# Two interleaved recurrences: products that use the same weights share one weight load on TensorE

## What is computed

```
# layer 1, state h1 (2 x 256), for each position
gate = sigmoid(h1 @ Wh + x_t @ Wz + b)
h1 = tanh(h1 * leak + gate * x_t)
# layer 2, a gated recurrent unit, state h2 (2 x 256), for each position
z  = sigmoid(x_t @ W_z + h2 @ U_z + bias_z)
r  = sigmoid(x_t @ W_r + h2 @ U_r + bias_r)
hh = tanh(x_t @ W + (r * h2) @ U + bias_h)
h2 = (1 - z) * h2 + z * hh
```

## Time and profile before

| | before |
|---|---|
| time, median of 3 runs | 2874.2 us |
| span of the profiled execution | 2951.0 us |
| TensorE matmul records | 2645.3 us, 90% of the span, 61812 of them |
| TensorE weight loads | 2205.5 us, 75%, 61812 of them |
| VectorE | 2060.0 us, 70% |
| ScalarE | 1601.3 us, 54% |
| chain that ended last | PE 79%, DVE 10%, ACT 4% |

### The profile page before, as it was taken

One profiled execution on the slowest core, in us unless ns is written; L12 is line 12 of the kernel. 1 busy time (PEld: TensorE's weight loads), 2 busy tenths in 40 slices (PEclk: granted clock), 3 DMA queues, 4 the chain that ended last, 5 costly groups with the idle time before them and its releaser, 6 DMA issues.

```text
span 2951.0 us, 154070 instructions
## 1 busy us (share of the span) xinstructions
PE 2645.3 (90%) x61812; PEld 2205.5 (75%) x61812; DVE 2060.0 (70%) x12247; ACT 1601.3 (54%) x8445; POOL 338.1 (11%) x457
## 2 busy tenths in 40 slices
PE   7579999999999999999999999989759999979994
PEld 5468888888888888888888888877647777744332
DVE  6788788876777777777777777756547776666228
ACT  3445565556666666666666666654335565521115
POOL 0000101001010010101001010010114444410000
PEclk7555555555555555555555555555559999979997
DMA  3132322212221222212212222220349777342000
GB/s 133 35 115 80 92 76 77 82 45 85 67 77 57 78 81 59 83 53 83 77 58 83 63 82 67 63 77 4 111 174 318 244 218 216 91 155 86 0 0 29
DMA packets 171242, 271.16 MB, mean 92 GB/s; under 512 B 23417, under 2 KB 127756, under 8 KB 168228
## 3 DMA queue, kind: packets, MB, share of 16 engines
q1 hardware_dynamic: 122852, 196.52, 21.3%
q10 hardware_dynamic: 32368, 31.12, 3.8%
q0 software_dynamic: 15312, 33.67, 3.4%
HBM read 170.77 MB, written 98.70 MB: 91 GB/s over the span
## 4 chain that ended last, share of the span: by engine, by line
PE 79%; DVE 10%; ACT 4%; issue 3%; SPq 2%; DMA 1%; POOL 0%; ACTq 0%; POOLq 0%; DVEq 0%
PE bank_r L737 7%; PE bank_r L746 7%; PE bank_g L737 6%; PE bank_h L737 6%; PE work L737 6%; PE bank_z L737 6%; PE work L727 5%; PE bank_h L746 4%; PE bank_g L746 3%; PE bank_z L746 3%; PE bank_z L965 3%; PE work L965 3%; PE work L988 2%; PE work L1074 2%; PE bank_h L988 2%
## 5 line engine op out<-in xcount | busy, mean ns | idle before, releaser
L737 PEld LDWEIGHTS work<-h_run,hi_r 128*128 128x128 f16 x4092 | 194.4, 108 | 218.9 <-DVE h_run L1887 165.6
L1872 DVE TENSOR_TENSOR_SCAN rh_run<-r_run,h_run 128x12 f16<-128x12 f32 x1023 | 187.4, 183 | 236.4 <-ACT r_run L1264 163.2
L737 PE MATMUL work<-h_run,hi_r 128*128 128x2 f16 x4092 | 275.0, 171 | 77.5 <-DVE h_run L1887 68.0
L1887 DVE TENSOR_TENSOR_SCAN h_run<-z_run,hh_run 128x12 f16<-128x12 f32 x1024 | 187.1, 183 | 222.6 <-ACT hh_run L1274 202.6
L1274 ACT ACTIVATE hh_run<-bank_h 128x4 f32<-128x4 f32 x1024 | 179.3, 175 | 295.2 <-PE bank_h L746 295.2
L746 PE MATMUL bank_h<-rh_run,hi_h 128*128 128x2 f16 x4092 | 258.5, 167 | 71.3 <-DVE rh_run L1872 70.8
L1255 ACT ACTIVATE r_guess<-work 128x4 f32<-128x4 f32 x1023 | 177.8, 174 | 215.3 <-PE work L737 203.9
L737 PE MATMUL bank_g<-h_hi,hi_g 128*128 128x2 f16 x4092 | 253.4, 166 | 43.9 <-ACT h_hi L1244 42.4
L737 PE MATMUL bank_h<-h_run,hi_h 128*128 128x2 f16 x4092 | 256.3, 167 | 0.9 <-DVE h_run L1869 0.7
L746 PE MATMUL bank_g<-h_lo,hi_g 128*128 128x2 f16 x4092 | 253.7, 166 | 2.3 <-issue 0.7
L1269 ACT ACTIVATE z_run<-bank_z 128x4 f32<-128x4 f32 x1024 | 179.5, 175 | 137.5 <-PE bank_z L746 7.4
(11 more groups left out here) (517 smaller groups left out, 7990.1 us busy)
## 6 DMA issues: line engine op xcount, KB each, us to landing
stage<-in_gate_up SPq DMA_DIRECT2D x128, 384.0 KB
stage<-in_down SPq DMA_DIRECT2D x128, 192.0 KB
gu_split<-parts SPq DMA_DIRECT2D x64, 384.0 KB
gu_ring<-gu_split SPq DMA_DIRECT2D x64, 384.0 KB
xt<-x_rows ACTq DMA_DIRECT2D x191, 128.5 KB
x_rows<-zero_rows SPq DMA_DIRECT2D x64, 257.0 KB, 3.1
yk<-y_rows SPq DMA_DIRECT2D x16, 1024.0 KB, 4.8
dn_split<-parts SPq DMA_DIRECT2D x64, 192.0 KB
```

Source lines behind the costliest of these rows:

```text
L737: ins = pe.matmul(o[:, m, step, :], w[:, k, m * P:(m + 1) * P], hi(k), start=False, stop=False, skip_group_check=True)
L1872: dve.tensor_tensor_scan(threes(t.rh_run), threes(t.r_run), t.h2_run[:, 2:2 + 3 * KH * B], 0.0, ALU.mult, ALU.subtract).then_inc(s.rhlo, 1)
L1887: dve.tensor_tensor_scan(t.h2_run[:, 0:3 * KH * B], threes(t.z_run), threes(t.hh_run), 0.0, ALU.mult, ALU.add).then_inc(s.h2hi, 1)
```

## The change

`again` issues a matmul without a weight load: it uses the weights that the matmul before it loaded. In `guess_products` each weight tile of the reset gate's hi part is loaded once and serves two matmuls, first the one into `bank_r`, then the one of the guess; the guess's semaphore `rg_mm` is raised by the last of the eight. In `hi_products` each hi tile serves the hi state and then the lo state, for the update gate and for the first recurrence. The number of matmuls stays as it was; 12 of 52 weight loads of a step with both recurrences go.

```
+    def again(out, w, x):
+        ins = mybir.InstMatmult(name=pe.bass.get_next_instruction_name(), engine=mybir.EngineType.PE,
+                                ins=[pe.lower_ap(x), pe.lower_ap(w)], outs=[pe.lower_ap(out)], ldweights=False,
+                                start_tensor_calc=False, stop_tensor_calc=False, tile_size=(P, P), tile_position=(0, 0),
+                                bass_skip_group_check=True)
+        return pe.add_instruction(ins)
+
+    def guess_products(c, step, hi):
+        guess, r = gate_cols(t.bank_of["guess"], c), gate_cols(t.r, c)
+        for m in range(KH):
+            for k in range(KH):
+                w = t.hi["r"][:, k, m * P:(m + 1) * P]
+                pe.matmul(r[:, m, step, :], w, hi(k), start=False, stop=False, skip_group_check=True)
+                ins = again(guess[:, m, step, :], w, hi(k))
+        return ins
+
+    def hi_products(g, c, step, hi, lo):
+        o = gate_cols(t.bank_of[g], c)
+        for m in range(KH):
+            for k in range(KH):
+                w = t.hi[g][:, k, m * P:(m + 1) * P]
+                pe.matmul(o[:, m, step, :], w, hi(k), start=False, stop=False, skip_group_check=True)
+                ins = again(o[:, m, step, :], w, lo(k))
+        return ins
...
-            big_products(t.bank_of["guess"], t.hi["r"], c2, s2, h2_hi).then_inc(s.rg_mm, 1)
-            big_products(t.r, t.hi["r"], c2, s2, h2_hi)
+            guess_products(c2, s2, h2_hi).then_inc(s.rg_mm, 1)
             big_products(t.r, t.lo["r"], c2, s2, h2_hi)
             pe.wait_ge(s.h2lo, t2)
             small_products("r", c2, s2, h2_lo).then_inc(s.r_mm, 1)
-            big_products(t.z, t.hi["z"], c2, s2, h2_hi)
             big_products(t.z, t.lo["z"], c2, s2, h2_hi)
-            small_products("z", c2, s2, h2_lo).then_inc(s.z_mm, 1)
+            hi_products("z", c2, s2, h2_hi, h2_lo).then_inc(s.z_mm, 1)
...
             if t1 > 0:
                 pe.wait_ge(s.h1hi, t1)
-                big_products(t.g1, t.hi["g1"], c1, s1, h1_hi)
+                big_products(t.g1, t.lo["g1"], c1, s1, h1_hi)
+                if not t2:
+                    big_products(t.g1, t.hi["g1"], c1, s1, h1_hi)
         if t2:
             pe.wait_ge(s.rhlo, t2)
             small_products("h", c2, s2, rh_lo).then_inc(s.h_mm, 1)
-        if t1:
-            big_products(t.g1, t.lo["g1"], c1, s1, h1_hi)
...
             pe.wait_ge(s.h1lo, t1)
-            small_products("g1", c1, s1, h1_lo).then_inc(s.g_mm, 1)
+            if t2:
+                hi_products("g1", c1, s1, h1_hi, h1_lo).then_inc(s.g_mm, 1)
+            else:
+                small_products("g1", c1, s1, h1_lo).then_inc(s.g_mm, 1)
```

## The result

The changed kernel takes **2937.5 us** (2935.5 to 2941.0, 4 runs) against 2874.7 us for the kernel before in the same comparison: a ratio of 1.022, 95% interval 1.021 to 1.024. That is 63 us slower; 61 were forecast. The profiled execution has a span of 2936.3 us, which agrees with its timed runs, as the first trace of the kernel before did not.

What follows compares the result with a forecast made beforehand. A latency ring was taken as the bound, each step set by when the candidate's last set starts. Delaying the guess adds 809 x 0.075 = 61 us, other terms zero: 2935 us, range 2850 to 2957.

Steps and rivals of the forecast that it cites:

- The price of a load-free matmul: TensorE: a matmul using weights already loaded takes as long as a whole load and matmul pair, 0.0268 us.
- The three rows: Profile evidence that matmul distance hardly depends on clock, load width or weights being ready, so the price is near 0.0268 us.
- The free case: Rival: a matmul without a load slips in beside the next load at no cost; 2854 us, chance 0.18.
- the half price: Rival: load and matmul share the pair's distance evenly, 0.0134 us per load-free matmul; about 2881 us, chance 0.11.
- the dearer matmul: Rival: a load-free matmul costs more than a pair, at 0.035 us giving 2963 us; chance 0.04.
- The guess: Second recurrence: its last matmul becomes eighth, its sigmoid starts 0.107 us later, the candidate 0.09 later; mean loss 0.075 in 809 steps.
- The wait: TensorE, line 1869: a new wait for the guess's multiplication, 0.09 us in some 800 steps.
- The two zeros: Sharing loads in the update gate (1023 steps) and the first recurrence (922 steps) changes the time by zero.
- The lone steps: 101 steps of the second recurrence alone: 0.12 us to spare before the candidate's last set, over 0.09, so zero loss.
- The steps with a transfer: 113 steps paired with GpSimd's indirect transfer: the full gate's sigmoid starts 0.74 us late, so a later guess costs nothing.
- the other case: If the timed runs lack the 113 stalls, those steps lose as well: 922 x 0.075 = 69 us.
- The sum: Whole kernel: 809 steps x 0.075 us = 61 us added, median 2935 us, 2.1% slower.

Runs made afterwards that it cites:

- the block: Kernel before plus unused matmuls into a free bank, with and without loads at several widths, after the recurrences and after the experts: 2872.8 us, a single run.
- the run that fills it: The change with the first recurrence's lo set moved ahead of the candidate and of TensorE's wait for the guess: 2914.0 us, ratio 1.014.
- second trace of before: The kernel before, unchanged, run and profiled once more: 2871.2 us, span 2872.4, ratio 0.999 to the kernel before beside it.

## Why the prediction was right

*The price of a load-free matmul.* Taken as 0.0268 us, the upper end; measured 0.025. The three rows it rested on (full clock, narrow weights, the record that begins before its weights are there) pointed the right way, and the block shows it directly. The first of them was weaker than it was read: (0.24 - 0.17) / 3 is 0.023 and not 0.024, and a set of four at half clock in the trace of before has the same 0.24:

```profile
1000.46 0.24 PE L737 MATMUL bank_r<-h_run,lo_r 128*128 128x2 f16 x4
```

The two clocks differ by less than the rows' last digit there, and only the sixteen in a row tell them apart. The free case (2854), the half price (2881) and the dearer matmul (2963) are out: load-free matmuls of two columns are not closer than 0.025 us. The shared sets take 0.21 us for eight matmuls, and neither 0.11 nor more than before.

*The guess.* Sigmoid at 0.41, candidate at 0.84 and 1.16, a step of 1.91: each as forecast. Both halves of the step's reason are shown by runs: the order without the sharing costs as much, and one matmul less ahead of the guess's end gives 23 us.

*The wait.* Forecast as a row of waits at line 1869 of 0.09 us in some 800 steps. It isn't listed as such, since the matmul records overlap it; it shows in the starts, 28 matmuls and 0.84 us where 0.75 would do, and in the run that fills it. The two matmul starts on either side of it are about 0.10 us apart, where a stream has 0.027, in some 900 of the 922 steps, so it is 0.07 us long, in more steps than were forecast.

*The two zeros.* Update gate and first recurrence were put at zero; without them the change costs the same, 2938.3 against 2937.5. Beside the late guess that is right within the measurement; without it they gave 6 to 8 us, which the zero did not have.

*The lone steps, put at zero, are a miss.* The row of before showed 0.12 us to spare between the candidate's sets and its last one, and I took the scan as waiting for the full gate alone. It also waits for the multiplication of the guess (`rhhi`). A lone step of the change:

```profile
2145.50 0.18 PE L764 MATMUL bank_r<-h_run,hi_r 128*128 128x2 f16 x1 [0.48 <-DVE h_run L1916]
...
2146.11 0.17 DVE L1898 SCALAR_TENSOR_TENSOR h_run<-r_guess,h 128x4 f16<-128x4 f32 x1 [0.38 <-ACT r_guess L1284]
...
2146.39 0.18 DVE L1901 TENSOR_TENSOR_SCAN rh_run<-r_run,h_run 128x12 f16<-128x12 f32 x1
...
2146.62 0.26 PE L746 MATMUL bank_h<-rh_run,hi_h 128*128 128x2 f16 x4
...
2147.37 0.16 PEld L764 LDWEIGHTS bank_r<-h_run,hi_r 128*128 128x128 f16 x2 [0.57 <-DVE h_run L1916]
```

The multiplication ends at 2146.28, the scan starts 0.11 later, and the candidate's last set 1.12 us into the step in place of 1.07. The step takes 1.87 to 1.88 where it took 1.82 to 1.83; over the 101 steps the mean rose from 1.829 to 1.885 (second trace of before), 6 us in all.

*The steps with a transfer, put at zero, are the other miss.* I took their stalls from the first trace as part of the schedule, and named the other case (922 x 0.075 = 69) without taking it. They are not part of it: in the second trace of before those steps take 1.879 us on average, and in the change's 1.923. They lose 0.04 each, 5 us.

*The sum.* The recurrences' part of the trace, first to last scan, is 1973.0 us in the change and 1908.1 in the second trace of before:

```profile
L1916 DVE TENSOR_TENSOR_SCAN h_run<-z_run,hh_run x1024: 169/182/184, 189.2 to 2162.2; 128x12 f16<-128x12 f32 x171
```

```profile
L1887 DVE TENSOR_TENSOR_SCAN h_run<-z_run,hh_run x1024: 168/182/184, 189.2 to 2097.3; 128x12 f16<-128x12 f32 x171
```

That is 65 us more. By the starts of these scans it falls into 6 us in the lone steps, 5 in the steps with a transfer, and 54 in the other 810, 0.067 each. The median step rose by 0.086 (1.827 to 1.913), as the 0.09 of the prediction had it. The mean is lower for two reasons. In some steps a busy VectorE hides a part, as forecast. And the change's trace has fewer long steps, 26 over 2.1 us holding 10 us above a median step against 42 holding 23, which the prediction did not have; these 13 us left out, the mean rise of the 922 steps is 0.079. So the 0.075 was the right size, and the 61 came near the measured 63 because two terms left out (11 us) and fewer long steps (13 us) nearly cancel. The mechanism was right, the exactness of the sum was luck. Every trace with a changed order or with shared loads has 22 to 28 such steps, the second trace of before and the one with the blocks, whose recurrences are those of before, have 42 and 36; whether that comes with the order stays open.

## What to carry to other kernels

A weight load that lies beside its matmul is hardly a cost: count matmuls, not loads, where the moving side is a few columns (2 to 16 here), because each matmul holds its place for 0.025 us with or without one, and the load adds under 0.002. When two products are interleaved to share something, ask which of them is waited for first; its last matmul moves back by the length of the other, and in a ring with several paths that end together even 0.02 us of slack is all there is. And check a profiled span against the timed runs before taking stalls from it: a second trace here lacked 111 of 119 of them.

## What was not expected of the hardware

- The place of a matmul of up to 16 columns is 0.025 us at half clock and at full clock alike, though 16 columns at 1.2 GHz are 0.013. At 32 columns, the next width run, half clock shows (0.027, and 0.053 for 64: from 2106.40 to 2107.25, 0.85 over sixteen).
- VectorE's scan starts 0.10 to 0.11 us behind the end of the instruction on the same engine whose result it waits for, where it starts 0.02 to 0.03 us behind ScalarE's.
- One execution of an unchanged kernel had 119 waits of ScalarE that took 86 us together, nearly all beside GpSimd's indirect transfers; the second profiled execution had 8.
